# Soft mixture of experts: slot products ahead of both experts' halves, a mix in 32-column blocks, the tokens' maxima moved into the steps

## The chip, the cores and the metric

One core of one Trainium2 chip runs the whole kernel as one launch. The metric is the device time of one execution in microseconds (us); below a time is the median of its runs.

## The reference, cut to what matters

The kernel computes four pairs of attention and feed-forward layers on 32 batches of 64 tokens (2048 tokens) of 128 features. The change touches one of the eight, the soft mixture of experts of the third pair, on 64 experts with 32 slots each (2048 slots):

```python
logits = jnp.einsum('bmd,dnp->bmnp', x, phi)              # 32 x 64 tokens, 64 experts, 32 slots
dispatch = jax.nn.softmax(logits, axis=0)                 # over the 32 batches
combine = jax.nn.softmax(logits.reshape(bsz, m, n * p), axis=-1).reshape(bsz, m, n, p)
slots = jnp.einsum('bmd,bmnp->bnpd', x, dispatch)
y = jnp.einsum('bnpd,nde->bnpe', slots, W) + b[None, :, None, :]
out = jnp.einsum('bnpd,bmnp->bmd', y, combine)
```

`x` is the normalised input, and `out` is added to the residual. The softmax of `dispatch` needs, for each position and slot, a maximum over the 32 batches; that of `combine` needs one maximum for each token over all 2048 slots. The tokens lie in 16 tiles of 128 (two batches each).

## The kernel before, in words

`soft_moe` has the five engines as five programs, each in its own written order, joined by counting semaphores; an engine waits at each instruction whose data or buffer isn't ready, and everything behind it on that engine waits too. It works in `I` = 8 chunks of 256 slots (8 experts). In chunk `i`:

- The stage of logits. TensorE computes the logits of the chunk ahead, j = i + 1, in eight products `logits(j, k)` (L1794) of two token tiles each into the two banks `slot_ps`, and between them transposes chunk i's weights `comb` (`turn`, L1816). ScalarE copies each out of its bank (`take_logits` L1927, `take_turned` L1931). VectorE's `survey(j, k)` takes the tokens' maxima by a reduction (L2063) and the slots' running maxima `high` by an elementwise maximum against the bank (L2055). `conclude` (L2071 to L2076) folds them into `tall`, `neg` (minus the running maximum of each token over the chunks so far) and `gap` (the step of it).
- Eight steps of slots, g = 0 to 7, one for each pair of token tiles. `fill_slots(i, g)` (L1833) makes the slots' inputs into both `slot_ps` banks; ScalarE copies them out (`take_slots`, L1939); `experts(i, g, c)` (L1847) multiplies with the weights of four experts, c = 0 and 1 being the two halves; VectorE adds the bias (`take_experts`, L2129); `mix(i, g)` (L1861) sums the experts' outputs for the tokens, and VectorE's `add` (L2145) adds that to `acc` with the rescaling of earlier chunks.
- Inside the steps the chunk ahead is prepared: ScalarE's `exp_comb(j, k)` (L1949), four exponentials with sums, k = 0 to 3; GpSimd's `lower(j, k)` (L2019), which subtracts the slots' maxima `peak`; ScalarE's `exp_spread(j, k)` (L1959); VectorE's `add_up` (L2109); then `swap_part` (L1808), `invert`, and GpSimd's four `share` (L2024) in the stage of logits.

`fill_slots(i, g)` waits until `take_slots(i, g - 1)` is through, `experts(i, g, c)` until the slots are copied and the bank's last content is taken, `mix(i, g)` until both halves have their bias. TensorE's order in the steps is

```python
for g in range(1, 8):
    experts(i, g - 1, 0)
    if g == (1 if i else 2) and ahead:
        swap_tall(i + 1)
    fill_slots(i, g)
    experts(i, g - 1, 1)
    if g >= 2:
        mix(i, g - 2)
```

The last chunk has nothing ahead; VectorE's `invert_tokens` (L2152 to L2159), small operations on 128x16, stands between `add(i - 1, 7)` and its steps.

Of the kernel before, what the change touches and what calls it, by code (L numbers as in the profile page):

```python
# [1711 lines left out]
def soft_moe(nc, core):  # L1712
# [7 lines left out]
    with Step(nc, "soft") as st:  # L1720
# [48 lines left out]
        wide = lambda v: v[:].unsqueeze(1).broadcast_to([128, 4, SC])  # L1769

# [11 lines left out]
        def _(pe):  # L1782
            def logits(j, k):
                if k >= 2:
                    pe.wait_ge(logit_taken, 8 * j + k - 1)
                    if j >= 2 and k >= 3:
                        pe.wait_ge(high_step, 7 * j + k - 2)
                elif j >= 2:
                    pe.wait_ge(slot_taken, 8 * (j - 1))
                elif j == 1:  # L1790
                    pe.wait_ge(logit_taken, 8)
                for tt in range(2):
                    t = 2 * k + tt
                    last = nc.tensor.matmul(slot_ps[k % 2][:, tt, :], core.xnT[:, 128 * t:128 * t + 128],  # L1794
                                            phi[:, 2 * j:2 * j + 2, :], start=True, stop=True)
                last.then_inc(logit_done, 1)
# [55 lines left out]
            def mix(i, g):  # L1852
# [5 lines left out]
                for tt in range(2):  # L1858
                    for c in range(2):
                        for h in range(2):  # L1860
                            last = nc.tensor.matmul(mix_ps[64 * h:64 * h + 64, tt, :],  # L1861
                                                    combT[:, c, 2 * g + tt, 64 * h:64 * h + 64], outs[u % 3][:, c, h, tt, :],
                                                    start=(c == 0), stop=(c == 1))
# [16 lines left out]
            for i in range(I):  # L1880
# [9 lines left out]
                if i:  # L1890
                    mix(i - 1, 7)
# [30 lines left out]
        def _(act):  # L1922
            def take_logits(j, k):
# [3 lines left out]
                nc.scalar.activation(spread[j % 2][:, 2 * k:2 * k + 2, :], slot_ps[k % 2][:], ACT.Copy).then_inc(logit_taken, 1)  # L1927
# [25 lines left out]
            def exp_gap(j):  # L1953
                act.wait_ge(gap_done, j)
# [22 lines left out]
            for i in range(I):  # L1977
# [8 lines left out]
                for g in range(8):  # L1986
# [3 lines left out]
                    if ahead:  # L1990
# [56 lines left out]
        def _(dve):  # L2047
# [9 lines left out]
            def survey(j, k):  # L2057
# [3 lines left out]
                if j >= 2:  # L2061
                    heighten(j, k, slot_ps[k % 2][:])
# [4 lines left out]
            def conclude(j):  # L2067
# [3 lines left out]
                nc.vector.tensor_tensor(tall[:], high[:, 0, :], high[:, 1, :], ALU.max).then_inc(tall_done, 1)  # L2071
                dve.wait_ge(own_done, 8 * j + 8)
# [121 lines left out]
            for i in range(I):  # L2194
# [6 lines left out]
                if i and ahead:  # L2201
                    survey(i + 1, 0)
                    survey(i + 1, 1)
                if i:
                    add(i - 1, 7)
                if i and ahead:
                    for k in range(2, 8):
                        survey(i + 1, k)
                    conclude(i + 1)
                if not ahead:  # L2210
                    invert_tokens()
                for g in range(1, 8):
                    take_experts(i, g - 1, 0)
                    if g == (1 if i else 2) and ahead:
                        take_peak(i + 1)
# [399 lines left out]
```

## Time and profile before

| | |
|---|---|
| median of 3 runs | 1032.79 us (1032.47 to 1032.89) |
| span of the profiled execution, first to last instruction | 1031.8 us |
| profiled execution's time outside its span | not recorded; the runs' median is 1.0 us above the span |
| mean granted TensorE clock | 0.942 of full speed |
| soft mixture, first `swap_part` to last `mix` | 542.9 to 913.1 us |
| one whole chunk inside it | 46.8 us |

The page gives each engine's busy share over the span; views of a stretch give the same for one stage, and the timeline gives the instructions in the order of time. Columns of a timeline row are start, length, engine, line, operation, output and input with their shapes, the number merged into the row, and in brackets the idle time before it with what ended it. A row that merges many matmuls ends when the last has drained, which overlaps the start of the next.

### The profile page before, as it was taken

How to read it: one execution, taken by the hardware profiler on the slowest of the kernel's cores; microseconds unless marked ns; L12 is line 12 of the kernel's file. 1: busy time of each engine (PE TensorE's matmuls, PEld its weight loads, DVE VectorE, ACT ScalarE, POOL GpSimd, SP SyncE). 2: the span in 40 equal slices, each digit the busy share in tenths (PEclk: the TensorE clock that was granted, in tenths of full speed). 3: DMA queues.
4: the chain of work that ended last, by engine and by line, in shares of the span. 5: the costliest groups of instructions: out<-in, count | busy, mean ns of one | idle time of the engine just before them, and what ended most of it. 6: DMA issues, size and time to landing. Idle time of an engine off the chain costs nothing. (4 is left out here: it accounts for less than half of the span.)

```text
span 1031.8 us, 26604 instructions
## 1 busy us (share of the span) xinstructions
PE 857.6 (83%) x10453; PEld 625.7 (61%) x10453; DVE 749.6 (73%) x1825; ACT 572.7 (56%) x1316; POOL 437.1 (42%) x286
## 2 busy tenths in 40 slices
PE   4274798889739996889878999999999999878888
PEld 3152554778526775545556777777777776644567
DVE  4989787678765544688797758576776758589974
ACT  4172244567615553467687484756648484246774
POOL 5000220597226776198205343342516253509820
PEclk9587899899959999899979999999999999899999
DMA  5411000400051112200010000000000000000001
GB/s 161 123 50 82 1 1 1 171 2 2 17 223 46 52 52 63 59 1 2 3 50 2 27 3 27 3 27 3 27 15 14 28 2 3 2 2 1 2 2 41
DMA packets 27127, 35.95 MB, mean 35 GB/s; under 512 B 7835, under 2 KB 20444, under 8 KB 26238
## 3 DMA queue, kind: packets, MB, share of 16 engines
q1 hardware_dynamic: 21310, 27.84, 8.4%
q0 software_dynamic: 2496, 5.12, 1.8%
q8 instruction: 85, 1.39, 0.6%
q10 hardware_dynamic: 3200, 1.31, 0.5%
q14 instruction: 36, 0.29, 0.1%
HBM read 26.98 MB, written 7.27 MB: 33 GB/s over the span
## 5 line engine op out<-in xcount | busy, mean ns | idle before, releaser
L2129 DVE TENSOR_TENSOR soft_outs<-soft_expert_ps,soft_bias 128x512 f32<-128x512 f32 x128 | 87.3, 688 | 89.5 <-PE soft_expert_ps L1847 89.5
L1847 PE MATMUL soft_expert_ps<-soft_W,soft_slots 128*32 128x128 f32 x4096 | 138.4, 278 | 9.7 <-issue 4.5
L1847 PEld LDWEIGHTS soft_expert_ps<-soft_W,soft_slots 128*32 128x32 f32 x4096 | 106.0, 110 | 40.7 <-issue 37.3
L1939 ACT ACTIVATE soft_slots<-soft_slot_ps 128x512 f32<-128x512 f32 x128 | 69.5, 594 | 85.2 <-PE soft_slot_ps L1833 83.5
L953 POOL TENSOR_TENSOR l_prob<-l_prob,l_inv 128x1024 f32<-128x1024 f32 x48 | 91.3, 1901 | 40.4 <-DVE l_inv L1107 39.0
L2024 POOL TENSOR_TENSOR l_ring<-l_ring,soft_inv 128x1024 f32<-128x1024 f32 x15 | 35.1, 2373 | 106.2 <-DVE soft_inv L2122 57.7
L1092 DVE TENSOR_REDUCE l_under<-l_score 128x16 f32<-128x1024 f32 x48 | 58.8, 1224 | 26.7 <-PE l_score L1173 14.4
L1794 PE MATMUL soft_slot_ps<-phi,xnT 128*128 128x256 f32 x256 | 69.3, 408 | 7.4 <-ACT soft_spread L1927 4.7
L1861 PE MATMUL soft_mix_ps<-soft_outs,soft_combT 128*64 128x128 f32 x1024 | 70.1, 279 | 1.5 <-DVE soft_acc L2145 1.5
L982 PE MATMUL l_turned<-ident,l_prob 128*128 128x128 f32 x384 | 52.4, 279 | 21.9 <-POOL l_prob L953 21.9
L1056 ACT ACTIVATE l_probT<-l_turned 128x512 f32<-128x512 f32 x96 | 52.1, 594 | 33.2 <-PE l_turned L982 33.2
L2024 POOL TENSOR_TENSOR soft_spread<-soft_spread,soft_inv 128x1024 f32<-128x1024 f32 x16 | 37.4, 2372 | 73.9 <-DVE soft_inv L2122 73.9
L1861 PEld LDWEIGHTS soft_mix_ps<-soft_outs,soft_combT 128*64 128x64 f32 x1024 | 54.7, 137 | 15.4 <-issue 13.8
L982 PEld LDWEIGHTS l_turned<-ident,l_prob 128*128 128x128 f32 x384 | 41.1, 140 | 33.5 <-POOL l_prob L953 33.3
L1794 PEld LDWEIGHTS soft_slot_ps<-phi,xnT 128*128 128x128 f32 x256 | 48.0, 202 | 18.0 <-ACT soft_spread L1927 5.8
L1101 DVE TENSOR_REDUCE l_total<-l_prob 128x16 f32<-128x1024 f32 x48 | 58.0, 1208 | 0.1
L1351 POOL DMA_INDIRECT xn_tok<-moe_rows,expert_source x39 | 37.8, 970 | 44.3 <-DVE expert_target L1588 32.7
L2019 POOL TENSOR_TENSOR soft_spread<-soft_spread,soft_peak 128x1024 f32<-128x1024 f32 x16 | 37.9, 2377 | 27.7 <-ACT l_values L1949 27.7
L1096 DVE TENSOR_TENSOR l_shifted<-l_score,l_under 128x768 f32<-128x768 f32 x48 | 46.0, 957 | 1.6
L1493 ACT ACTIVATE expert_rings<-expert_turned 128x512 f32<-128x512 f32 x39 | 23.3, 597 | 42.2 <-PE expert_turned L1394 42.2
L1355 POOL DMA_INDIRECT moe_back<-xnT,expert_target x39 | 38.4, 985 | 19.0 <-DVE xnT L1616 10.4
L1046 ACT ACTIVATE l_prob<-l_shifted 128x768 f32<-128x768 f32 x48 | 40.6, 845 | 10.6 <-DVE l_shifted L1096 10.6
(450 smaller groups left out, 2174.4 us busy)
## 6 DMA issues: line engine op xcount, KB each, us to landing
moe_w<-in_moe_W SPq DMA_DIRECT2D x2, 2048.0 KB, 10.1
soft_W<-in_soft_W SPq DMA_DIRECT2D x16, 256.0 KB, 2.8
kept<-early SPq DMA_DIRECT2D x1, 2048.0 KB, 6.3
l_keys<-in_moe_b SPq DMA_DIRECT2D x1, 2048.0 KB, 8.2
l_asked<-kept SPq DMA_DIRECT2D x1, 2048.0 KB, 13.0
ctxT<-in_ctxT SPq DMA_DIRECT2D x1, 1024.0 KB, 5.1
moe_rows<-xn_tok SPq DMA_DIRECT2D x4, 256.0 KB, 3.7
expert_rings<-moe_back SPq DMA_DIRECT2D x4, 256.0 KB, 6.1
```

The lines of the kernel that those rows point to most:

```text
L953: nc.gpsimd.tensor_tensor(prob[t % 4][:], prob[t % 4][:], inv[t % 2][:].unsqueeze(2).broadcast_to(S16), ALU.mult).then_inc(share_done, 1)
L982: last = nc.tensor.transpose(turned[j][:, k, :], prob[t % 4][:, 2 * m:2 * m + 2, :], core.ident[:])
L1056: nc.scalar.activation(probT[t % 2][:, 4 * j:4 * j + 4, :], turned[j][:], ACT.Copy).then_inc(done, 1)
L1092: nc.vector.tensor_reduce(under[t % 2][:], scores[t % 2][:], AX.X, ALU.max, negate=True).then_inc(top_done, 1)
L1096: nc.vector.tensor_tensor(shifted[t % 2][:], scores[t % 2][:, 0:KEEP, :], under[t % 2][:, 0:KEEP].unsqueeze(2).broadcast_to([128, KEEP, S] ...
L1101: nc.vector.tensor_reduce(total[t % 2][:], prob[t % 4][:], AX.X, ALU.add).then_inc(total_done, 1)
L1794: last = nc.tensor.matmul(slot_ps[k % 2][:, tt, :], core.xnT[:, 128 * t:128 * t + 128], phi[:, 2 * j:2 * j + 2, :], start=True, stop=True)
L1847: last = nc.tensor.matmul(expert_ps[c][32 * j:32 * j + 32, h, tt, :], slots[u % 3][:, h, tt, 128 * c + 32 * j:128 * c + 32 * j + 32], W[i ...
L1861: last = nc.tensor.matmul(mix_ps[64 * h:64 * h + 64, tt, :], combT[:, c, 2 * g + tt, 64 * h:64 * h + 64], outs[u % 3][:, c, h, tt, :], sta ...
L1939: last = nc.scalar.activation(slots[u % 3][:, h], slot_ps[h][:], ACT.Copy)
L2024: nc.gpsimd.tensor_tensor(spread[j % 2][:, quarter(k), :], spread[j % 2][:, quarter(k), :], wide(inv), ALU.mult).then_inc(share_done, 1)
L2129: nc.vector.tensor_tensor(outs[u % 3][:, c].rearrange("p h t d -> p (h t) d"), expert_ps[c][:].rearrange("p h t d -> p (h t) d"), bias[i % ...
```

## The change

Four edits in `soft_moe`, for chunks i >= 1 unless said otherwise:

1. In each step `fill_slots(i, g)` comes first, then both experts' halves of g - 1, then `mix(i, g - 2)` (all chunks). `mix` is cut into blocks of 32 columns: 32 weight loads and matmuls in place of 16.
2. `mix(i - 1, 7)` moves from the start of the stage of logits to behind `fill_slots(i, 0)`, and `swap_tall(i + 1)` to behind `turn(i, 7)`.
3. Logits of later chunks go through four banks: `slot_ps` and, for k % 4 >= 2, `expert_ps`.
4. VectorE keeps only the slots' maxima in the stage of logits (`survey_slots`, `heighten_last`). The tokens' maxima move into the steps: `survey_tokens(i + 1, g)` for g = 0 to 3, each with its quarter of `neg` and `gap`. `exp_comb(i + 1, g)` now waits for its own quarter; `exp_gap` and `exp_spread` come one step later.

```diff
 # TensorE
-                if k >= 2:
+                if j >= 2:
+                    if k >= 4:
+                        pe.wait_ge(logit_taken, 8 * j + k - 3)
+                        if k >= 5:
+                            pe.wait_ge(high_step, 7 * j + k - 4)
+                    elif k >= 2:
+                        pe.wait_ge(expert_taken, 16 * (j - 2) + 15 + k - 2)
+                    else:
+                        pe.wait_ge(slot_taken, 8 * (j - 1))
+                elif k >= 2:
                     pe.wait_ge(logit_taken, 8 * j + k - 1)
...
-                        for h in range(2):
-                            last = nc.tensor.matmul(mix_ps[64 * h:64 * h + 64, tt, :],
-                                                    combT[:, c, 2 * g + tt, 64 * h:64 * h + 64], outs[u % 3][:, c, h, tt, :],
-                                                    start=(c == 0), stop=(c == 1))
+                        for j in range(4):
+                            last = nc.tensor.matmul(mix_ps[32 * j:32 * j + 32, tt, :],
+                                                    combT[:, c, 2 * g + tt, 32 * j:32 * j + 32], outs[u % 3][:, c, j // 2, tt, :],
+                                                    start=(c == 0), stop=(c == 1), tile_position=(0, 32 * j))
...
                 if i:
-                    mix(i - 1, 7)
                     for k in range(7):
...
                 fill_slots(i, 0)
+                if i:
+                    mix(i - 1, 7)
                 turn(i, 7)
+                if i and ahead:
+                    swap_tall(i + 1)
                 for g in range(1, 8):
+                    fill_slots(i, g)
                     experts(i, g - 1, 0)
-                    if g == (1 if i else 2) and ahead:
-                        swap_tall(i + 1)
-                    fill_slots(i, g)
                     experts(i, g - 1, 1)
                     if g >= 2:
                         mix(i, g - 2)
+                    if g == 2 and not i:
+                        swap_tall(1)
 # ScalarE
-                elif k == 0:
-                    act.wait_ge(neg_done, j + 1)
-                    act.wait_ge(turn_done, 8 * j)
+                else:
+                    act.wait_ge(neg_done, neg_by(j, k))
+                    if k == 0:
+                        act.wait_ge(turn_done, 8 * j)
...
-                        if h == 0:
+                        if h == (4 if i else 0):
                             exp_gap(i + 1)
-                        if 2 <= h < 6:
-                            exp_spread(i + 1, h - 2)
+                        low = h - 3 if i else h - 2
+                        if 0 <= low < 4:
+                            exp_spread(i + 1, low)
 # VectorE
+            def survey_tokens(j, k):
+
+                survey(j, 2 * k)
+                survey(j, 2 * k + 1)
+                dve.wait_ge(own_done, 8 * j + 2 * k + 2)
+                nc.vector.tensor_tensor(neg[:, j, quarter(k)], neg[:, j - 1, quarter(k)], own[:, j, quarter(k)], ALU.min).then_inc(neg_done, 1)
+                dve.wait_ge(neg_done, neg_by(j, k))
+                nc.vector.tensor_tensor(gap[:, j, quarter(k)], neg[:, j, quarter(k)], neg[:, j - 1, quarter(k)], ALU.subtract).then_inc(gap_done, 1)
...
                 if i and ahead:
-                    survey(i + 1, 0)
-                    survey(i + 1, 1)
+                    for k in range(8):
+                        survey_slots(i + 1, k)
+                    heighten_last(i + 1)
                 if i:
                     add(i - 1, 7)
                 if i and ahead:
-                    for k in range(2, 8):
-                        survey(i + 1, k)
-                    conclude(i + 1)
+                    survey_tokens(i + 1, 0)
+                    take_peak(i + 1)
...
+                    if i and ahead and g < 4:
+                        survey_tokens(i + 1, g)
```

## Rows read from the trace of the kernel before

**Rows 1.** The page, busy time of each engine over the whole span.
```profile
PE 857.6 (83%) x10453; PEld 625.7 (61%) x10453; DVE 749.6 (73%) x1825; ACT 572.7 (56%) x1316; POOL 437.1 (42%) x286
```

**Rows 2.** Windows, seven steps of one chunk: length, busy (instructions) by engine, clock, DMA, GB/s.
```profile
690.00:723.70 33.70, 32.89 (x694) 25.19 (x694) 19.56 (x40) 20.88 (x54) 9.50 (x4) 1.00 0.01 3
```

**Rows 3.** Timeline, TensorE: start, length, engine, line, operation; `swap_part` of two chunks.
```profile
676.93 0.70 PE L1808 MATMUL soft_swap_ps<-soft_part,halves 128*128 128x256 f32 x2
...
723.74 0.70 PE L1808 MATMUL soft_swap_ps<-soft_part,halves 128*128 128x256 f32 x2
```

**Rows 4.** Timeline, TensorE, one step of slots.
```profile
707.48 1.09 PE L1861 MATMUL soft_mix_ps<-soft_outs,soft_combT 128*64 128x128 f32 x16
708.50 1.08 PE L1847 MATMUL soft_expert_ps<-soft_W,soft_slots 128*32 128x128 f32 x32
709.51 1.13 PE L1833 MATMUL soft_slot_ps<-soft_spread,xn_tok 64*128 64x256 f32 x8
710.58 1.08 PE L1847 MATMUL soft_expert_ps<-soft_W,soft_slots 128*32 128x128 f32 x32
711.59 1.09 PE L1861 MATMUL soft_mix_ps<-soft_outs,soft_combT 128*64 128x128 f32 x16
```

**Rows 5.** Timeline, TensorE, both experts' halves without a slot product between.
```profile
720.83 1.95 PE L1847 MATMUL soft_expert_ps<-soft_W,soft_slots 128*32 128x128 f32 x64
...
722.72 1.09 PE L1861 MATMUL soft_mix_ps<-soft_outs,soft_combT 128*64 128x128 f32 x16
```

**Rows 6.** Timeline, the stage of logits up to the first slot product.
```profile
724.28 1.89 PE L1794 MATMUL soft_slot_ps<-phi,xnT 128*128 128x256 f32 x8
...
732.84 1.03 PE L1794 MATMUL soft_slot_ps<-phi,xnT 128*128 128x256 f32 x4
...
733.71 0.60 PE L1816 MATMUL soft_turn_ps<-ident,l_values 128*128 128x128 f32 x4
...
734.14 1.03 PE L1794 MATMUL soft_slot_ps<-phi,xnT 128*128 128x256 f32 x4
...
735.84 0.69 DVE L2055 TENSOR_TENSOR soft_high<-soft_high,soft_slot_ps 128x512 f32<-128x512 f32 x1
...
736.67 1.13 PE L1833 MATMUL soft_slot_ps<-l_ring,xn_tok 64*128 64x256 f32 x8 [0.63 <-POOL l_ring L2024]
```

**Rows 7.** Timeline, ScalarE, one step with its exponentials.
```profile
702.47 1.09 ACT L1939 ACTIVATE soft_slots<-soft_slot_ps 128x512 f32<-128x512 f32 x2
...
703.45 0.51 ACT L1949 ACTIVATE l_values<-l_ring,soft_neg 128x256 f32<-128x256 f32 x1
...
705.41 1.05 ACT L1959 ACTIVATE l_ring<-l_ring 128x1024 f32<-128x1024 f32 x1
```

**Rows 8.** Timeline, VectorE: an addition, a reduction, the tokens' minimum.
```profile
712.73 0.61 DVE L2145 SCALAR_TENSOR_TENSOR soft_acc<-soft_acc,soft_scale,soft_mix_ps 128x128 f32<-128x128 f32 x2 [0.31 <-PE soft_mix_ps L1861]
...
729.93 0.68 DVE L2063 TENSOR_REDUCE soft_own<-soft_spread 128x2 f32<-128x512 f32 x1
...
730.52 0.68 DVE L2055 TENSOR_TENSOR soft_high<-soft_high,soft_slot_ps 128x512 f32<-128x512 f32 x1
...
737.37 0.17 DVE L2074 TENSOR_TENSOR soft_neg<-soft_neg,soft_own 128x16 f32<-128x16 f32 x1
```

**Rows 9.** Timeline, GpSimd's shares beside small VectorE operations.
```profile
867.70 9.33 POOL L2024 TENSOR_TENSOR soft_spread<-soft_spread,soft_inv 128x1024 f32<-128x1024 f32 x4 [19.22 <-DVE soft_inv L2122]
...
870.12 2.29 DVE L2155 TENSOR_TENSOR soft_token<-soft_token,soft_scale 128x16 f32<-128x16 f32 x1
```

**Rows 10.** Timeline and windows, TensorE after long idle time.
```profile
443.08 1.09 PE L982 MATMUL l_turned<-ident,l_prob 128*128 128x128 f32 x8 [1.66 <-POOL l_prob L953]
...
880.33 1.94 PE L1847 MATMUL soft_expert_ps<-soft_W,soft_slots 128*32 128x128 f32 x32 [3.32 <-DVE soft_outs L2129]
...
880.30:886.00 5.70, 5.67 (x72) 4.08 (x72) 1.17 (x2) 1.09 (x2) 5.50 (x6) 0.50 0.00 0
...
927.19 1.98 PE L1672 MATMUL l_score<-l_ring,xn_tok 64*64 64x512 f32 x8 [2.15 <-ACT l_prob L1048]
```

More of the change, by code:

```diff
@@ L1769, in soft_moe @@
         wide = lambda v: v[:].unsqueeze(1).broadcast_to([128, 4, SC])
+        apart = [bank[:].rearrange("p h t d -> p h (t d)") for bank in expert_ps]
+        logit_bank = lambda j, k: apart[k % 2] if j >= 2 and k % 4 >= 2 else slot_ps[k % 2][:]
+        neg_by = lambda j, k: j + 1 if j < 2 else 4 * (j - 2) + k + 3
+        gap_by = lambda j: j if j < 2 else 4 * (j - 1) + 1
         @block.sync
@@ L1783, in logits @@
             def logits(j, k):
-                if k >= 2:
+                if j >= 2:
[8 more added lines that the diff above has]
+                elif k >= 2:
                     pe.wait_ge(logit_taken, 8 * j + k - 1)
[L1786 to L1789, printed above, removed]
                 elif j == 1:
@@ L1793, in logits @@
                     t = 2 * k + tt
-                    last = nc.tensor.matmul(slot_ps[k % 2][:, tt, :], core.xnT[:, 128 * t:128 * t + 128],
+                    last = nc.tensor.matmul(logit_bank(j, k)[:, tt, :], core.xnT[:, 128 * t:128 * t + 128],
                                             phi[:, 2 * j:2 * j + 2, :], start=True, stop=True)
@@ L1926, in take_logits @@
                     act.wait_ge(slot_done, 8 * (j - 1))
-                nc.scalar.activation(spread[j % 2][:, 2 * k:2 * k + 2, :], slot_ps[k % 2][:], ACT.Copy).then_inc(logit_taken, 1)
+                nc.scalar.activation(spread[j % 2][:, 2 * k:2 * k + 2, :], logit_bank(j, k), ACT.Copy).then_inc(logit_taken, 1)
             def take_turned(i, k):
@@ L1953, in exp_gap @@
             def exp_gap(j):
-                act.wait_ge(gap_done, j)
+                act.wait_ge(gap_done, gap_by(j))
                 nc.scalar.activation(scale[:, j, :], gap[:, j, :], ACT.Exp).then_inc(scale_done, 1)
@@ L2060, in survey @@
                 dve.wait_ge(logit_taken, 8 * j + k + 1)
-                if j >= 2:
-                    heighten(j, k, slot_ps[k % 2][:])
                 nc.vector.tensor_reduce(own[:, j, 2 * k:2 * k + 2], here, AX.X, ALU.max, negate=True).then_inc(own_done, 1)
@@ L2065, in survey, with survey_slots, heighten_last @@
                     heighten(j, k, here)
-            def conclude(j):
+            def survey_slots(j, k):
+                dve.wait_ge(logit_taken, 8 * j + k + 1)
+                heighten(j, k, logit_bank(j, k))
+            def survey_tokens(j, k):
[5 more added lines that the diff above has]
+                nc.vector.tensor_tensor(gap[:, j, quarter(k)], neg[:, j, quarter(k)], neg[:, j - 1, quarter(k)], ALU.subtract).then_inc(gap_done, 1)
+            def heighten_last(j):
                 dve.wait_ge(high_step, 7 * j + 7)
@@ L2071, in conclude @@
                 nc.vector.tensor_tensor(tall[:], high[:, 0, :], high[:, 1, :], ALU.max).then_inc(tall_done, 1)
+            def conclude(j):
+                heighten_last(j)
                 dve.wait_ge(own_done, 8 * j + 8)
@@ L2213, in _ @@
                     take_experts(i, g - 1, 0)
-                    if g == (1 if i else 2) and ahead:
-                        take_peak(i + 1)
+                    if g == 2 and not i:
+                        take_peak(1)
                     if i == 0 and g == 1:
```

## The prediction

> **What bounds the kernel now.** I first read the busy shares of the page: TensorE is the busiest engine with 83%, VectorE follows with 73% [rows 1]. Those are averages over stages, so I went to the windows of the stage that the change touches. In the steps of one chunk TensorE is busy for 32.89 of 33.70 us at a granted clock of 1.00, VectorE for 19.56 and ScalarE for 20.88 [rows 2]: here TensorE is the bound, and only its own instructions, the gaps between them, or a wait put in their place can move the time. The timeline of TensorE then gives the frame: from one `swap_part` to the next 46.81 us [rows 3], of which 12.93 lie between `swap_part` and `fill_slots(i, 0)` [rows 3, 6] (the stage of logits), and so 33.88 from there to the next `swap_part` (the steps). Six chunks (i = 1 to 6) repeat this; the first and the last are special.
>
> A step takes 4.11 us [rows 4], start to start: experts to slots 1.01, slots to experts 1.07, experts to mix 1.01, and mix to experts 1.02. Two expert halves one behind the other take 1.89 until the mix starts, so 0.88 for the first and 1.01 for the second [rows 5]: leaving one shape of tile for another costs some 0.13 us.
>
> **The change part by part.** All sums are made against this execution, span 1031.8 us, which stands 1.0 us under the median of 1032.79; I carry differences over to the median.
>
> *Order in the steps and 32-column mix.* Slots, half, half, mix is 1.07 + 0.88 + 0.88 + 1.01 = 3.84 us, 0.27 less, if the mix follows the experts as one half follows the other and keeps TensorE as long. Its 32 pieces of 32 columns have the shape of one half of the experts, and a half and a 64-column mix take the same time now (1.01 and 1.02), so I take 0.88 + the switch. Bounds: no more than a mix and its switch today (1.02, so 0.14 more in each step that TensorE bounds), no less than 0.84, since the same columns stream. No trace row shows a mix of this shape. The Trainium skill (TensorEngine Tiling (Array Packing), Key Properties) says that a change of tiling mode drains the engine while a change of tile doesn't; by it, too, this mix would follow without a drain.
>
> *Stage of logits, chunks 1 to 6.* Now summed for after: `swap_part` to the first logits 0.54, two logits 1.73, five rounds of logits and transposes of 1.30 (732.84 to 734.14), and 2.53 from the last logits to the first slot product: its drain, ScalarE's copy, VectorE's maximum, which ends at 736.53 and releases `fill_slots` [rows 6]. Together 11.30 against 12.93: 1.6 us less for each chunk. This last wait stays as it is, since slot products still wait for all eight copies and maxima. What goes is `mix(i - 1, 7)` and its two switches, and a third of a microsecond of waiting for `high`. The third logits now wait for `take_experts(i - 1, 7, 0)`, over 1 us earlier by my schedule: nothing.
>
> *Maxima in the steps, chunks 1 to 6.* Here a new ring of waits closes. I count from the start of `fill_slots(i, g)`. TensorE starts `mix(i, g - 2)` 2.83 later and ends it at 3.92. Behind it VectorE adds from 3.97 (two instructions, 0.53 until the next can start), reduces twice (0.60 each to the next start, 0.68 for the last), and forms `neg` (0.17 and some 0.04 for the semaphore) [rows 8]: 5.98. `exp_comb(i + 1, g)` starts 0.04 later and holds ScalarE for 1.96 [rows 7]; only behind it stands `take_slots(i, g + 1)`, 1.09 [rows 7]; then `fill_slots(i, g + 2)` can start 0.13 later (as 735.84 + 0.69 to 736.67, [rows 6]). That is 9.2 us for two steps, 4.6 each, where TensorE needs 3.84 and the old order took 4.11. In the old order the exponentials waited for nothing inside the steps.
>
> GpSimd makes it longer. `neg` and `gap` have both inputs in SBUF. Beside GpSimd's four shares (2.33 each) such an operation of 128x16 took 2.29 us, ending where the current share ended; with GpSimd idle it takes 0.17 [rows 8, 9]. In the steps `lower(i + 1, k)` (L2019) has a share's shape, which I take at a share's 2.33, and starts about 0.2 behind `exp_comb(i + 1, k)`, so the next `neg` is out no earlier than 2.56 behind those exponentials. The Trainium skill (SBUF — State Buffer, Who interferes with whom) gives this as a rule: a VectorE instruction with two SBUF inputs contends with GpSimd's reads, and the later one blocks fully. The trace agrees; if it did not hold here, the sum below would be 0.7 us a chunk shorter.
>
> The schedule, from the start of `fill_slots(i, 0)`: `mix(i - 1, 7)` 1.07, `turn` 2.10, `swap_tall` 2.54, `fill_slots(1)` 3.17, experts 4.24 and 5.12. VectorE: `add(i - 1, 7)` 2.21, the first `neg` 4.24. (`tall` stands behind the last share until about 1.6; `swap_tall` needs it at 2.5: hidden under the mix, 0.) `exp_comb(0)` 4.28 to 6.36; `take_slots(1)` 6.25 to 7.34; `fill_slots(2)` 7.47, where TensorE was ready at 6.13. `neg(1)` would be out at 8.36 and is held by `lower(0)` until 8.92; `exp_comb(1)` ends at 11.04, `fill_slots(3)` 12.15. The same again, 4.68 later each: `fill_slots(4)` 16.83, `exp_comb(3)` ends 20.40. Behind it `exp_spread(0)` takes 1.04 more [rows 7] before `take_slots(4)`, so `fill_slots(5)` 22.55, where TensorE was ready at 20.7. From there TensorE bounds: 3.84 each, `fill_slots(7)` 30.23, then slots, four halves and two mixes 6.47 to `swap_part` at 36.70. `add_up(0)` is held by `lower(3)` until about 23.4, VectorE is needed again at 24.7: 0. Against 33.88 this is **2.8 us more** for each chunk.
>
> *First chunk.* No ring, the tokens' maxima stay where they were. Five clean steps give 5 x 0.27 = 1.35; the chain to `swap_part` goes over `add(0, 5)`, whose mix now stands one half (0.76 net) later behind its slots: 0.6 to 0.8 less.
>
> *Last chunk.* `invert_tokens` now stands behind an `add(6, 7)` that comes after the slot product. Of it the first operations wait for share ends either way [rows 9], so the stall of TensorE, which ended at 880.33, ends some 0.4 later. But the next slot product, 2.0 us at the half clock of 0.50 behind that stall [rows 10], now runs ahead of it, and four or five steps save 0.27: 2.4 less, with 0.3 lost in VectorE's tail.
>
> *Sum:* 6 x (2.8 - 1.6) - 0.7 - 2.4 = +4.1: span 1035.9, median **1036.9 us**.
>
> **The rivals.** *The ring is shorter than my sum.* If `neg` slips in ahead of `lower`, or semaphores are quicker, a chunk loses 0.7 us of what I add: 6 x 0.7 = 4.2, 1032.7, no change. For it: my `neg` 2 and 3 miss a free GpSimd by only 0.1 to 0.2. Against: [rows 9]. *It doesn't bind (the other side).* If two steps of the ring took 7.68 or less, 1.5 below my count, TensorE would bound all steps: 3.17 + 2.96 + 5 x 3.84 + 6.47 = 31.8, so 2.1 less than 33.88 in each chunk; with 1.6 from the logits 6 x 3.7 + 3.1 = 25 us less, 1007. It decides at `take_slots(i, g + 1)`; half of that shortening would give some 1022. Against it stands that each part of the ring has its row. *The clock falls.* Ahead of `fill_slots(5)` TensorE idles for about 1.8 us. Behind 1.66 us of idling its matmuls kept their length (1.09 for eight), behind 2.15 and 3.32 they took twice that, and the clock was 0.50 for 5.7 us behind the latter [rows 10], 2.9 lost. In all six chunks that is 17 us: 1054; in one or two, 1040 to 1043. TensorE doing less than I think in the steps makes that likelier. *The 32-column mix is not quicker.* 0.14 in some 28 to 35 steps that TensorE bounds: 4 to 5 us, 1041.
>
> **Chances.** The forecast 0.56 (own range 1033 to 1041, which is 0.7 us a chunk either way); the shorter ring 0.14; not binding 0.12; clock 0.12; mix not quicker 0.06. The range 1029 to 1045 holds the forecast, the shorter ring, the mix, and single falls of the clock; it leaves out most of "not binding" and the full loss of clock. Within 0.2% (1030.7 to 1034.9, about what a measurement of this kernel can tell from no change) lie the shorter ring and a little of the forecast: 0.19. Slower: the rest of the forecast, clock, mix, 0.67. Faster 0.14.
>
> **What would show it.** In the trace after: steps 5 to 7 of a chunk at 3.84 us; `swap_part` to the first slot product 11.3; in steps 1 to 4 `exp_comb` waiting for `neg`, `take_slots` late behind it with nothing to wait for, and `fill_slots` waiting for ScalarE, starts 4.7 apart; `neg` operations of 0.5 us and more instead of 0.17; GpSimd's `lower` 4.7 apart. TensorE's busy share in the steps falls to about 85%. Wrong it would be if VectorE got through its reductions before the mix, if `exp_comb` were out of the way sooner, or if a clock below 1.00 stood in the windows of chunks 1 to 6.

## Result and the profile after

Slower, by about as much as its measurement can tell: 1035.88 us (median of 13 runs, 1034.50 to 1037.33) against 1033.36 us for the kernel before (13 runs, 1032.31 to 1035.70), a ratio of 1.0023 with a 95% interval of 1.0014 to 1.0031. The profiled execution has a span of 1032.5 us and its own time is 1034.5 us, the lowest of the 13. So the spans of the two profiled executions lie only 0.7 us apart where the medians lie 2.5 apart; what follows accounts for the 0.7.

In the profile of the changed kernel the lines of `soft_moe` stand some 9 lines (TensorE) to 29 (end of VectorE's program) further down. First the page of the changed kernel, its busy time by engine:

```profile
PE 832.9 (81%) x11477; PEld 630.6 (61%) x11477; DVE 780.2 (76%) x1861; ACT 572.7 (55%) x1316; POOL 436.4 (42%) x286
```

TensorE has 1024 more instructions and 24.7 us less busy time than in [rows 1]. Of these, 21.3 us lie between the first `swap_part` and the next layer's first scores (357.0 before, 335.7 now). Most of that is the 0.29 us by which TensorE's own work in each of the 64 steps became shorter (3.82 for 4.11), through fewer switches of tile shape; a smaller part is matmuls that ran at half clock before and no longer do. Yet the time did not fall. The windows of one chunk of the changed kernel say where it went, first the steps, then the stage of logits:

```profile
688.70:725.00 36.30, 31.82 (x838) 26.99 (x838) 29.58 (x55) 21.07 (x55) 11.26 (x5) 1.00 0.01 3
677.38:688.68 11.30, 10.67 (x66) 9.30 (x63) 8.49 (x14) 8.08 (x15) 7.48 (x4) 1.00 0.19 58
```

In the steps before, TensorE worked for 32.89 of 33.70 us [rows 2]; now it works for 31.82 of 36.30 and is no longer what bounds them. VectorE has some 10 us more work in the steps (29.58 for 19.56), mostly the reductions that moved there. The granted clock is 1.00 in both. The timeline of the changed kernel over that chunk (compare [rows 3, 4, 6, 7]) shows what TensorE waits for:

```profile
677.38 0.70 PE L1817 MATMUL soft_swap_ps<-soft_part,halves 128*128 128x256 f32 x2
...
688.68 1.13 PE L1842 MATMUL soft_slot_ps<-soft_spread,xn_tok 64*128 64x256 f32 x8 [0.63 <-DVE soft_high L2069]
...
691.78 1.13 PE L1842 MATMUL soft_slot_ps<-soft_spread,xn_tok 64*128 64x256 f32 x8
...
695.15 2.35 POOL L2033 TENSOR_TENSOR l_ring<-l_ring,soft_peak 128x1024 f32<-128x1024 f32 x1 [4.61 <-ACT l_values L1962]
...
696.11 1.14 PE L1842 MATMUL soft_slot_ps<-soft_spread,xn_tok 64*128 64x256 f32 x8 [1.31 <-ACT soft_slots L1951]
696.77 0.75 DVE L2089 TENSOR_TENSOR soft_neg<-soft_neg,soft_own 128x4 f32<-128x4 f32 x1
...
697.55 0.51 ACT L1962 ACTIVATE l_values<-l_ring,soft_neg 128x256 f32<-128x256 f32 x1 [1.59 <-DVE soft_neg L2089]
...
699.53 1.05 ACT L1951 ACTIVATE soft_slots<-soft_slot_ps 128x512 f32<-128x512 f32 x2
699.77 2.37 POOL L2033 TENSOR_TENSOR l_ring<-l_ring,soft_peak 128x1024 f32<-128x1024 f32 x1 [2.27 <-ACT l_values L1962]
...
700.73 1.14 PE L1842 MATMUL soft_slot_ps<-soft_spread,xn_tok 64*128 64x256 f32 x8 [0.73 <-ACT soft_slots L1951]
701.90 0.26 DVE L2089 TENSOR_TENSOR soft_neg<-soft_neg,soft_own 128x4 f32<-128x4 f32 x1
...
705.37 1.14 PE L1842 MATMUL soft_slot_ps<-soft_spread,xn_tok 64*128 64x256 f32 x8 [0.75 <-ACT soft_slots L1951]
...
710.95 1.14 PE L1842 MATMUL soft_slot_ps<-soft_spread,xn_tok 64*128 64x256 f32 x8 [1.68 <-ACT soft_slots L1951]
...
714.77 1.14 PE L1842 MATMUL soft_slot_ps<-soft_spread,xn_tok 64*128 64x256 f32 x8
...
725.03 0.70 PE L1817 MATMUL soft_swap_ps<-soft_part,halves 128*128 128x256 f32 x2
```

Read it as a ring. The bracket of a slot product (L1842) names ScalarE's copy of the slots (L1951) as what it waited for. But that copy, at 699.53, has no wait of its own: it stands behind four exponentials, whose first (697.55) waited 1.59 us for `neg` (L2089). `neg` ended at 697.52, right where GpSimd's `lower` of the round before ended (695.15 + 2.35 = 697.50), and the next `neg` at 702.16 where the next `lower` ended (699.77 + 2.37 = 702.14). One round is 4.64 us. The hold itself is long only in the first round: `neg` took 0.75, 0.26 and 0.27 us for 0.16, so in the later two it was held for 0.1 us only. From 710.95 on the slot products are 3.82 us apart. All of it together, the idle time ahead of the slot products in the whole kernel (us, times):

```profile
its engine sat idle before it (us, times) until:
...
  ACT soft_slots L1951: 28.1, 25
```

That is four times in each of the six chunks, and once more. The last chunk, timeline of the changed kernel (against [rows 10]):

```profile
879.80 1.14 PE L1842 MATMUL soft_slot_ps<-soft_spread,xn_tok 64*128 64x256 f32 x8
...
884.80 2.52 PE L1856 MATMUL soft_expert_ps<-soft_W,soft_slots 128*32 128x128 f32 x64 [3.87 <-DVE soft_outs L2158]
887.03 2.00 PE L1870 MATMUL soft_mix_ps<-soft_outs,soft_combT 128*32 128x128 f32 x32
888.96 1.36 PE L1842 MATMUL soft_slot_ps<-soft_spread,xn_tok 64*128 64x256 f32 x8
```

Now the slot product (879.80) runs ahead of the stall, at full clock, and the half clock behind it costs 1.7 us (2.52, 2.00 and 1.36 for what takes 1.95, 1.06 and 1.14 elsewhere) where it cost 2.9.

| part, profiled executions | before | after | difference |
|---|---|---|---|
| up to the first `swap_part` | 542.88 | 542.61 | -0.27 |
| first chunk | 40.45 | 39.67 | -0.78 |
| six chunks | 280.85 | 285.70 | +4.85 (47.6 for 46.8 each) |
| last chunk, to the next layer's first scores | 57.81 | 54.86 | -2.95 |
| from there to the end | 109.8 | 109.7 | -0.15 |

### The profile page after: what moved, and what is told of

It reads as the page before. It is cut to its first block and busy times, and to the rows that moved or that the text cites. A ratio compares the mean times of both kernels' runs of the same rounds, so it can differ in the third digit from the quotient of the medians.

```text
span 1032.5 us, 28676 instructions
## 1 busy us (share of the span) xinstructions
PE 832.9 (81%) x11477; PEld 630.6 (61%) x11477; DVE 780.2 (76%) x1861; ACT 572.7 (55%) x1316; POOL 436.4 (42%) x286
## 5 line engine op out<-in xcount | busy, mean ns | idle before, releaser
L1856 PE MATMUL soft_expert_ps<-soft_W,soft_slots 128*32 128x128 f32 x4096 | 125.7, 275 | 4.8 <-DVE soft_outs L2158 4.8
L1856 PEld LDWEIGHTS soft_expert_ps<-soft_W,soft_slots 128*32 128x32 f32 x4096 | 108.9, 110 | 23.6 <-issue 23.6
L1951 ACT ACTIVATE soft_slots<-soft_slot_ps 128x512 f32<-128x512 f32 x128 | 68.6, 586 | 54.5 <-PE soft_slot_ps L1842 54.5
L1870 PE MATMUL soft_mix_ps<-soft_outs,soft_combT 128*32 128x128 f32 x2048 | 69.1, 275 | 1.0 <-DVE soft_acc L2174 1.0
L1870 PEld LDWEIGHTS soft_mix_ps<-soft_outs,soft_combT 128*32 128x32 f32 x2048 | 57.7, 111 | 3.7 <-issue 3.6
L1842 PE MATMUL soft_slot_ps<-l_ring,xn_tok 64*128 64x256 f32 x256 | 36.3, 400 | 17.6 <-ACT soft_slots L1951 14.8
L1842 PE MATMUL soft_slot_ps<-soft_spread,xn_tok 64*128 64x256 f32 x256 | 36.5, 402 | 16.0 <-ACT soft_slots L1951 13.2
L1803 PE MATMUL soft_slot_ps<-phi,xnT 128*128 128x256 f32 x160 | 43.6, 419 | 6.5 <-ACT soft_spread L1939 4.6
```

What stands on the lines that cost most here:

```text
L1842: last = nc.tensor.matmul(slot_ps[h][:, tt, :], core.xn[rows, t, :], spread[i % 2][rows, t, :], start=True, stop=True)
L1856: last = nc.tensor.matmul(expert_ps[c][32 * j:32 * j + 32, h, tt, :], slots[u % 3][:, h, tt, 128 * c + 32 * j:128 * c + 32 * j + 32], W[i ...
L1870: last = nc.tensor.matmul(mix_ps[32 * j:32 * j + 32, tt, :], combT[:, c, 2 * g + tt, 32 * j:32 * j + 32], outs[u % 3][:, c, j // 2, tt, :] ...
L1951: last = nc.scalar.activation(slots[u % 3][:, h], slot_ps[h][:], ACT.Copy)
```

## The experiments

A chunk below is the time from one `swap_part` to the next, in the middle of the stage. All ratios are to the kernel before, run on the same chip. The chunk is the cleaner of the two measures. In four of the profiled executions (64-column mix; exponentials a step later; both of the last two; `gap` by quarters) the granted clock fell to between 0.78 and 0.87 for the 30 us behind the next layer's first scores, and from those scores to the end they took 112.4 to 112.6 us, where all others took 109.7 to 110.2. Whether these falls belong to the edits isn't shown, so up to 2.9 us of a difference in time may lie outside the stage. The first of these stretches of 10 us in the kernel with the 64-column mix (window: length, busy by engine, clock):

```profile
912.12:922.12 10.00, 6.78 (x55) 3.65 (x56) 8.68 (x9) 4.56 (x11) 4.92 (x3) 0.78 0.00 1
```

| kernel | median us | ratio to before (95%) | one chunk us |
|---|---|---|---|
| before | 1033.36 | 1 | 46.81 |
| the change | 1035.88 | 1.0023 (1.0014 to 1.0031) | 47.65 |
| order and mix alone | 1015.46 | 0.9829 (0.9814 to 0.9844) | 44.70 |
| the same, 64-column mix | 1026.33 | 0.9927 (0.9910 to 0.9944) | 45.59 |
| change, all maxima back in the stage of logits | 1015.48 | 0.9825 (0.9808 to 0.9842) | 44.25 |
| change, exponentials a step later | 1022.13 | 0.9892 (0.9876 to 0.9907) | 44.97 |
| change, maxima into PSUM | 1031.85 | 0.9980 (0.9971 to 0.9989) | 46.99 |
| change, maxima ahead of the addition | 1034.40 | 1.0009 (0.9996 to 1.0022) | 47.64 |
| both of the last two | 1028.45 | 0.9951 (0.9934 to 0.9967) | 46.20 |
| exponentials later, PSUM, `gap` once | 1007.74 | 0.9745 (0.9729 to 0.9762) | 42.90 |
| exponentials later, PSUM, `gap` by quarters | 1010.95 | 0.9775 (0.9758 to 0.9791) | 43.28 |
| later, PSUM, `gap` once, and `invert_tokens` later | 1018.12 | 0.9844 (0.9828 to 0.9861) | 42.90 |
| the same, and GpSimd waits for it | 1019.20 | 0.9720 (0.9705 to 0.9734) | 42.90 |

### Which part of the change does what

*The step order and the 32-column mix alone*, in the kernel before; maxima, banks and `mix(i - 1, 7)` stay as they were:

```diff
-                        for h in range(2):
...
+                        for j in range(4):
...
                 turn(i, 7)
+                if i and ahead:
+                    swap_tall(i + 1)
                 for g in range(1, 8):
+                    fill_slots(i, g)
                     experts(i, g - 1, 0)
-                    if g == (1 if i else 2) and ahead:
-                        swap_tall(i + 1)
-                    fill_slots(i, g)
                     experts(i, g - 1, 1)
...
```

> The kernel before with the first edit alone: in each step the slot product first, then both experts' halves, then the mix in 32-column blocks; swap_tall behind turn(i, 7). Maxima, two banks and mix(i - 1, 7) stay as before. My theory (the order gains, the ring of waits in the steps eats it): the exponentials wait for nothing here, so steps run at 3.82 us, fill_slots(i, 0) to swap_part falls from 33.9 to about 31.4, the stage of logits stays at 12.9, a chunk 44.3; time 1015 us. Rival (the 32-column mix or the new order itself costs): steps at 4.1 us or more, time 1033 or above.

1015.46 us. A chunk is 2.11 us shorter, the six together 13.0; the first chunk gives 0.8 (39.68), the last 5.2 (850.77 to 903.38), and 0.8 is lost outside them. The steps came out as expected (31.5), the stage of logits at 13.2 us for 12.9. This part of the change is worth 18 us.

*The same with the old two blocks of 64 columns in `mix`:*

```diff
-                        for j in range(4):
-                            last = nc.tensor.matmul(mix_ps[32 * j:32 * j + 32, tt, :],
...
+                        for h in range(2):
+                            last = nc.tensor.matmul(mix_ps[64 * h:64 * h + 64, tt, :],
```

> The kernel before with the new order in the steps but its old mix in two 64-column blocks. My theory: the switch between the experts' shape and the mix's costs 0.13 us each time and there are 8 to 9 more of them in a chunk, so a step is 3.96 instead of 3.82 us, a chunk 45.8 instead of 44.7, time 1024 (the same order with 32 columns: 1015.5). Rival (the blocks don't matter, the order alone gains): 1015 to 1016.

1026.33. Timeline of this kernel, one step:

```profile
665.29 1.95 PE L1847 MATMUL soft_expert_ps<-soft_W,soft_slots 128*32 128x128 f32 x64
667.17 1.09 PE L1861 MATMUL soft_mix_ps<-soft_outs,soft_combT 128*64 128x128 f32 x16
668.20 1.13 PE L1833 MATMUL soft_slot_ps<-l_ring,xn_tok 64*128 64x256 f32 x8
669.26 1.96 PE L1847 MATMUL soft_expert_ps<-soft_W,soft_slots 128*32 128x128 f32 x64
```

and the same step of the changed kernel:

```profile
715.83 1.95 PE L1856 MATMUL soft_expert_ps<-soft_W,soft_slots 128*32 128x128 f32 x64
717.60 1.06 PE L1870 MATMUL soft_mix_ps<-soft_outs,soft_combT 128*32 128x128 f32 x32
718.59 1.13 PE L1842 MATMUL soft_slot_ps<-soft_spread,xn_tok 64*128 64x256 f32 x8
```

From the experts to the mix it takes 1.88 us against 1.77, from the mix to the slots 1.03 against 0.99. The mix in the experts' shape follows them 0.11 us sooner, and the slots follow it 0.04 sooner: 3.97 against 3.82 a step. A chunk is 0.89 us longer, the six together 5.6. The rest of the difference of about 10 (0.9927 less 0.9829, of 1033.4) lies in the first chunk (0.7), in the last (54.71 against 52.61, where the clock fell, see below), and in the next layer: 2.2 us in the profiled executions, with a granted clock of 0.78, 0.84 and 0.87 in the three stretches of 10 us behind its first scores, against 1.00, 0.83 and 1.00 with the 32-column mix. By an estimate from these rows some 7 us of the difference come from the shape itself, and 3 to 4 stand beside the lower clock (1.5 of them at the row of 3.47 us shown at the end); whether the shape brings the lower clock about isn't shown.

*The change with all the maxima back in the stage of logits* (four banks, order, mix and the place of `mix(i - 1, 7)` kept; `exp_gap` and `exp_spread` go back to their old steps with them):

```diff
-                    heighten_last(i + 1)
+                        survey(i + 1, k)
+                    conclude(i + 1)
...
-                    survey_tokens(i + 1, 0)
...
-                    if i and ahead and g < 4:
-                        survey_tokens(i + 1, g)
```

> The changed kernel with the tokens' maxima back in the stage of logits (all eight reductions and one neg there, exponentials as before), order, four banks, 32-column mix and mix(i - 1, 7) as changed. My theory: VectorE now paces the stage of logits (1.2 us for each of eight), swap_part to the first slot product 11.95 instead of 11.30, but no ring in the steps: 32.2 instead of 36.35, a chunk 44.1, time 1014. Rival (something else in the changed order costs): the steps stay at 35 or more, time 1033 or above.

1015.48, and a chunk of 44.25. Taken as differences between neighbouring kernels, the chunk's +0.84 has three parts: order and mix -2.11, four banks with the later `mix(i - 1, 7)` -0.45, tokens' maxima in the steps +3.40. The last is +4.27 in the steps (36.35 for 32.08) and -0.86 in the stage of logits (11.30 for 12.16). Six times 3.40 is 20.4 us, and the timed medians differ by the same 20.4; the profiled spans differ by 18.7, since this kernel's stage began 1.9 us later in its execution. Of the 2.5 that the banks gain in the six chunks against the first experiment, 2.05 were lost in the last chunk (54.66 for 52.61, a stall of 3.89 with the half clock behind it); the timed medians are equal.

### What closes the ring

Two closed chains of waits were possible. One goes over TensorE: mix, addition, maxima, `neg`, exponentials, copy of the slots, slot product. The other does without it: `neg`, exponentials, `lower`, which holds up the next `neg`.

*Maxima into PSUM*: the reductions of quarters 1 to 3 write to `swap_ps`, so `neg` has one input in SBUF and one in PSUM.

```diff
-                nc.vector.tensor_reduce(own[:, j, 2 * k:2 * k + 2], here, ...
+                nc.vector.tensor_reduce(swap_ps[:, 0, 2 * k:2 * k + 2] if j >= 2 and k >= 2 else own[...], here, ...
...
+                if k:
+                    dve.wait_ge(peak_done, j + 1)
```

> The changed kernel with the tokens' maxima of quarters 1 to 3 written to PSUM (the first half of swap_ps, free behind peak), so that the minimum for neg has one input in SBUF and one in PSUM; gap stays as it is. If GpSimd's lower holds up an operation with two SBUF inputs: neg takes 0.17 us instead of 0.75, 0.26 and 0.27, the ring is 0.8 us shorter in a chunk, chunk 46.85, 4.7 us less than the changed kernel, 1031. Rival (neg is late for another reason): no change, 1036. If the hold were the whole loss of the steps, fill_slots(i, 0) to swap_part would fall to 32; my theory says it stays near 35.5.

1031.85. Timeline of this kernel:

```profile
695.58 2.36 POOL L2033 TENSOR_TENSOR l_ring<-l_ring,soft_peak 128x1024 f32<-128x1024 f32 x1 [4.60 <-ACT l_values L1962]
...
696.54 1.13 PE L1842 MATMUL soft_slot_ps<-soft_spread,xn_tok 64*128 64x256 f32 x8 [1.31 <-ACT soft_slots L1951]
697.22 0.16 DVE L2091 TENSOR_TENSOR soft_neg<-soft_neg,soft_swap_ps 128x4 f32<-128x4 f32 x1
...
705.71 1.13 PE L1842 MATMUL soft_slot_ps<-soft_spread,xn_tok 64*128 64x256 f32 x8 [1.23 <-ACT soft_slots L1951]
```

`neg` takes 0.16 us in the middle of `lower`, so the hold came from its second input in SBUF. The chunk is 0.66 shorter, where the prediction gave 0.7. But from 696.54 to 705.71 two steps still take 9.17 us. The longer chain, over TensorE, was counted at 9.2 in the prediction and is nearly as long as two rounds of the other (9.28). Taking one of them away shows the other.

*Maxima ahead of the addition* in VectorE's order, in steps 2 and 3, which shortens the chain over TensorE alone; as an edit of the change, and then on top of the maxima in PSUM:

```diff
+                    if i and ahead and g < 4:
+                        survey_tokens(i + 1, g)
                     if g >= 2:
...
-                    if i and ahead and g < 4:
-                        survey_tokens(i + 1, g)
```

> The changed kernel with survey_tokens(i + 1, g) ahead of add(i, g - 2) in steps 2 and 3 on VectorE. My theory: in the changed kernel neg(2) and neg(3) end when GpSimd's lower ends, so starting them 0.53 us sooner changes nothing: chunk 47.6, 1036. Rival (the addition is in the ring that sets the time): 0.5 us less a chunk, 47.1, 1033.

> The same order (survey_tokens ahead of the addition) on the kernel with the maxima in PSUM, which measured 1031.85 us and a chunk of 46.98. There GpSimd no longer holds neg. My theory: now the addition is in the ring, neg(3) comes 0.53 us sooner and with it the fifth slot product: chunk 46.45, 1028.7. Rival (something else holds the ring): chunk 46.98, 1032.

Alone it leaves the chunk at 47.64: the hold sets the pace. With the hold gone it takes 0.79 us off the chunk (46.99 to 46.20). That is more than the 0.53 expected, because the maxima then wait neither for the addition nor for the mix in front of it: from the step's last bias addition to its first reduction it was 1.39 us (699.63 to 701.02) and is 0.60 (696.74 to 697.34). The hold and the chain are both real, and each covers the other.

*Exponentials one step later*: ScalarE forms `exp_comb(i + 1, k)` behind the slots' copy of step k + 1, so nothing in the same step waits for them.

```diff
-                        h = g if i else g - 1
+                        h = g - 1
...
-                        if h == (4 if i else 0):
+                        if h == (3 if i else 0):
                             exp_gap(i + 1)
-                        low = h - 3 if i else h - 2
+                        low = g - 3
```

> The changed kernel with exp_comb(i + 1, k) one step later on ScalarE (behind take_slots(i, k + 1) instead of in front of it); VectorE and TensorE untouched, so the tokens' maxima stay in the steps and GpSimd still holds them up. My theory (what costs is that the copy of the slots stands behind exponentials that wait for neg): fill_slots no longer waits, fill_slots(i, 0) to swap_part 31.6 us instead of 36.35, a chunk 42.9, time 1007. Rival (VectorE's extra work in the steps, or GpSimd's hold on it, is the cost by itself): the chunk stays at 46 to 47.6, time 1030 to 1036.

1022.13, 15 us above what was expected. Timeline of this kernel:

```profile
691.44 2.38 POOL L2033 TENSOR_TENSOR l_ring<-l_ring,soft_peak 128x1024 f32<-128x1024 f32 x1 [5.62 <-ACT l_values L1962]
692.08 1.77 DVE L2089 TENSOR_TENSOR soft_neg<-soft_neg,soft_own 128x4 f32<-128x4 f32 x1
...
693.88 0.51 ACT L1962 ACTIVATE l_values<-l_ring,soft_neg 128x256 f32<-128x256 f32 x1 [1.59 <-DVE soft_neg L2089]
...
696.10 2.37 POOL L2033 TENSOR_TENSOR l_ring<-l_ring,soft_peak 128x1024 f32<-128x1024 f32 x1 [2.28 <-ACT l_values L1962]
...
696.99 1.50 DVE L2089 TENSOR_TENSOR soft_neg<-soft_neg,soft_own 128x4 f32<-128x4 f32 x1
...
698.52 0.51 ACT L1962 ACTIVATE l_values<-l_ring,soft_neg 128x256 f32<-128x256 f32 x1 [1.61 <-DVE soft_neg L2089]
...
699.44 1.96 PE L1856 MATMUL soft_expert_ps<-soft_W,soft_slots 128*32 128x128 f32 x64 [0.64 <-DVE soft_outs L2158]
```

The chain over TensorE is open now, and that gives 2.68 us a chunk (44.97 for 47.65). But the ring of the hold still runs at 4.64 (693.88 to 698.52): `neg` is held longer, 1.77 and 1.50 us, the exponentials wait as before, and VectorE's bias additions behind `neg` come late for TensorE (0.64 us at 699.44). My expectation had let go of that ring, which the prediction had written down.

*Both taken away, and `gap` formed once, in step 5*, when `lower` is through; and the same with `gap` left as it was:

```diff
...
-                nc.vector.tensor_tensor(gap[:, j, quarter(k)], neg[:, j, quarter(k)], neg[:, j - 1, quarter(k)], ALU.subtract)...
...
+                    if i and ahead and g == 5:
+                        dve.wait_ge(neg_done, neg_by(i + 1, 3))
+                        nc.vector.tensor_tensor(gap[:, i + 1, :], neg[:, i + 1, :], neg[:, i, :], ALU.subtract)...
```

> The changed kernel with three edits: exp_comb(i + 1, k) one step later on ScalarE, the tokens' maxima of quarters 1 to 3 in PSUM, and gap formed once for all 16 tiles in step 5 (exp_gap in step 6). With the exponentials alone moved, the trace showed another ring: neg waits for the end of lower(k - 1), exp_comb for neg, lower for exp_comb, 4.64 us a round. My theory: with both rings open TensorE bounds all steps at 3.82 us, fill_slots(i, 0) to swap_part 31.6, a chunk 42.9, time 1007 to 1009. Rival (VectorE's work in steps 1 to 3, 3.6 us each, is itself too much): a chunk of 44 or more, 1015 or more.

> Exponentials one step later and maxima of quarters 1 to 3 in PSUM, but gap in each quarter as in the changed kernel (two SBUF inputs, so GpSimd still holds it and the work behind it on VectorE). My theory: nothing on TensorE's path waits for gap, VectorE runs under 1 us late and has that much slack: chunk 42.9 to 43.1, 1008. Rival (any operation that GpSimd holds costs its hold): chunk 44.6 as with neg held, 1018 or more.

1007.74: TensorE bounds every step. Timeline of this kernel:

```profile
686.94 1.13 PE L1842 MATMUL soft_slot_ps<-soft_spread,xn_tok 64*128 64x256 f32 x8
...
690.76 1.14 PE L1842 MATMUL soft_slot_ps<-soft_spread,xn_tok 64*128 64x256 f32 x8
...
694.58 1.13 PE L1842 MATMUL soft_slot_ps<-soft_spread,xn_tok 64*128 64x256 f32 x8
```

3.82 us from `fill_slots(2)` on, and 31.60 from the first slot product to `swap_part`. That is the time that the prediction gave the rival "it doesn't bind" (1007). `gap` by quarters has both inputs in SBUF and is held in its turn: 1.58 us at 690.19 and 1.32 at 698.21, for 0.16. That costs 0.38 us a chunk (43.28, where I had expected 42.9 to 43.1), 2.3 in six; the time is 3.2 us longer (1010.95), and this is one of the executions with the lower clock in the next layer.

### The last chunk

In all these kernels TensorE stalls once in the last chunk, behind `invert_tokens`. *That block moved behind `take_experts` of step 1*, on top of the fastest kernel so far:

```diff
-                if not ahead:
-                    invert_tokens()
                 for g in range(1, 8):
...
+                    if not ahead and g == 1:
+                        invert_tokens()
```

> The kernel with both rings open (1007.74 us), and in the last chunk invert_tokens moved behind the bias additions of step 1 instead of ahead of them. There TensorE idled for 3.89 us behind the third slot product and ran the next three groups at half clock. My theory: GpSimd's shares are over by then, so the 16 small operations take 3.3 us beside TensorE's work; the idle time goes, the clock stays at 1.00: 3.9 + 2.8 = 6.7 us less, 1001. Rival (VectorE is late anyway and the idle time only moves): 1006 to 1008.

1018.12, worse by 10 us. Timeline of this kernel:

```profile
854.46 4.04 DVE L2181 COPY soft_token<-soft_sums 128x16 f32<-128x16 f32 x1
...
854.95 3.52 POOL L159 MEMSET l_values<- 128x4096 f32 x1
...
858.53 4.19 POOL L165 COPY l_values<-l_asked 64x1024 f32<-64x1024 f32 x4
858.74 0.90 DVE L2186 TENSOR_TENSOR soft_token<-soft_token,soft_sums 128x16 f32<-128x16 f32 x1
...
862.80 7.47 POOL L185 TENSOR_TENSOR l_ring<-l_asked,head_of 128x1024 f32<-128x1024 f32 x4
...
864.78 1.82 DVE L2184 TENSOR_TENSOR soft_token<-soft_token,soft_scale 128x16 f32<-128x16 f32 x1
...
871.91 3.64 PE L1856 MATMUL soft_expert_ps<-soft_W,soft_slots 128*32 128x128 f32 x64 [13.24 <-DVE soft_outs L2158]
```

I had expected 1001. The block now falls into GpSimd's next work. Its copy is out only when the share and the MEMSET behind it have both ended (858.47), and the small operations, 0.17 us alone, take up to 0.95 and 1.82 beside GpSimd's copies and products. TensorE idles for 13.24 us.

*The same, with GpSimd waiting until the block is through:*

```diff
             pool.wait_ge(turn_done, 8 * I)
+            pool.wait_ge(token_step, 2 * I)
             queries.lay_apart(pool)
```

> As the kernel with invert_tokens behind step 1's bias additions, which measured 1018.12 us, but GpSimd waits for the end of invert_tokens before it lays the next layer's queries apart (its memset, copies and products). In the trace of that kernel the copy of 128x16 took 4.04 us, until the memset ended, and eight of the small two-input operations 0.9 to 1.8 us each beside GpSimd's copies and products. My theory: it was only this company that cost; without it the operations take 3.4 us, TensorE idles under 1 us and keeps its clock: 6 us less than the kernel with both rings open (1007.74), 1001 to 1002. Rival (GpSimd's work, now 3 to 4 us later, delays the next layer, or its products hold up VectorE in later steps): 1006 to 1010.

On the chip that ran this one the kernel before took 1048.35 us (9 runs), and this kernel's first `swap_part` comes at 558.70, that of the fastest one at 544.11: the excess lies ahead of the stage. So only ratios compare, 0.9720 against 0.9745, about 2.6 us, with intervals that overlap a little: that it is faster is likely and not shown. Inside the profiles the last chunk takes 51.66 us (855.83 to 907.49) against 55.64 (841.19 to 896.83). Timeline of this kernel:

```profile
868.34 0.60 DVE L2182 COPY soft_token<-soft_sums 128x16 f32<-128x16 f32 x1
...
872.31 3.52 POOL L159 MEMSET l_values<- 128x4096 f32 x1 [3.40 <-DVE soft_token L2189]
872.85 1.95 PE L1856 MATMUL soft_expert_ps<-soft_W,soft_slots 128*32 128x128 f32 x64 [0.30 <-DVE soft_outs L2159]
...
876.26 1.85 DVE L2195 SCALAR_TENSOR_TENSOR x_tok<-soft_acc,soft_token,x_tok 128x128 f32<-128x128 f32 x2
```

The stall shrank to 0.30 us and the clock kept its level, 4.0 us less in the chunk; I had expected 6. GpSimd's work, put later, now holds up VectorE's last additions (1.85 us at L2195 beside GpSimd's copies, 0.61 without), and TensorE waits for VectorE later in the chunk, 1.34 us at 889.55.

## Why the prediction was right, point by point

*The number.* 1035.88 lies 1.0 us under the 1036.9 forecast, and part of that is luck. The sum gave +4.1 us; the medians moved by 2.5 and the profiled spans by 0.7. The sum was 2.2 us too high in the six chunks, 0.6 in the last, 0.1 in the first, and 0.4 of the difference lies outside the stage. Against that, I had added 1.0 us to come from span to median. The executions timed later show 1.8 us between time and span for the kernel before and 2.0 for the changed one, and the median before came out at 1033.36 for 1032.79. So the span forecast, 1035.9, was 2.0 us above that of the median execution (1033.9), and the short step to the median took half of it back.

*Direction and mechanism.* Right. The ring closed where it was said to, in steps 1 to 4 of each chunk, at 4.64 us a round for the 4.68 of the sum, with `exp_comb` waiting for `neg`, the slots' copy late behind it, and a last stall of 1.68 us ahead of `fill_slots(5)` (about 1.8 predicted).

*Order and mix, 3.84 us a step.* 3.82. Taking the mix at the experts' price was right; with 64 columns a step took 0.15 us more, which is the 0.14 of the bound and of the rival "not quicker".

*Stage of logits, 11.30.* 11.30 (677.38 to 688.68), the wait of 0.63 for the last maximum included.

*Maxima in the steps, +2.8 a chunk.* This is the term that was mis-sized: +2.5 (36.35 against 33.88). From `fill_slots(0)` the slot products came at 3.10, 7.43, 12.05, 16.69 and 22.27, where the sum had 3.17, 7.47, 12.15, 16.83 and 22.55: each round a little short. With the stage of logits the net is +0.84 a chunk for +1.2, 2.2 us in six.

*GpSimd's hold, 0.7 a chunk.* 0.66 when it was taken away, though `neg` was held for more than 0.5 us in one round of three only, where the prediction had named 0.5 and more as the sign. The rule of the Trainium skill (SBUF — State Buffer, Who interferes with whom), that an instruction with two SBUF inputs waits out GpSimd's, holds in these steps: 0.75 us for `neg` with both inputs in SBUF, 0.16 with one in PSUM. That either chain is almost as long as the other was in the numbers (9.2 for two steps, two rounds of 4.68) and I did not draw the consequence, that shortening one gives only as much as the other lets through. Without the hold a chunk lost 0.66 us, with the chain over TensorE shortened nothing, with both 1.45. With that chain opened outright it lost 2.68, with both opened 4.75.

*First and last chunk, -0.7 and -2.4.* -0.78 and -2.95. The stall of the last chunk ended 0.7 us later relative to `swap_part` (16.82 for 16.15), where I had said 0.4. The slot product ran ahead of it at full clock, as said, and with it went 0.9 of the 2.9 us that the half clock had cost [rows 10]. What the half clock cost behind the stall was 1.7 us, 0.3 less than the rest, which was not foreseen.

*The clock.* Kept in the six chunks at idle times of 1.68 us, as [rows 10] had it for 1.66. *The rival "not binding"* (0.12) was wrong for this kernel; opening the two chains gave its time to within 1 us, so the price of the ring was right from that side too.

## What to carry over

Before moving work into steps that another engine bounds, write down each closed chain of waits that it adds, over every engine, with the length of one round. Where two are nearly equal, price taking away both, not one. Here a VectorE operation of 0.16 us carried a ring because both its inputs lay in SBUF and GpSimd was busy; writing one input to PSUM, or forming `gap` where GpSimd's `lower` was through, took the hold away. And measure the parts of a change alone: here order, mix and banks together were worth 18 us, and the maxima in the steps cost 20.

## What had not been expected of the hardware

The clock did not go by the length of the idling alone. Ahead of experts' products in the last chunk it kept its level behind an idle time of 2.36 us in the kernel with order and mix alone (64 matmuls 1.95 us), and fell behind one of 2.35 us in the one with the 64-column mix (3.47 us). The granted clock was 1.00 in the former from 865 to 880, and 0.83 in the latter from 870 to 880. First the former, then the latter, from their timelines:

```profile
867.20 1.95 PE L1847 MATMUL soft_expert_ps<-soft_W,soft_slots 128*32 128x128 f32 x64 [2.36 <-DVE soft_outs L2131]
```

```profile
873.55 3.47 PE L1847 MATMUL soft_expert_ps<-soft_W,soft_slots 128*32 128x128 f32 x64 [2.35 <-DVE soft_outs L2131]
```

The same shows in the next layer. Behind 2.15 us of idling a group of eight score matmuls took 1.98 us in the kernel before [rows 10], behind 2.14 in the changed one 1.09, from its timeline:

```profile
928.04 1.09 PE L1672 MATMUL l_score<-l_ring,xn_tok 64*64 64x512 f32 x8 [2.14 <-ACT l_prob L1048]
```

What tells them apart stays open; no run was made for it.

The copy of 128x16 from SBUF to SBUF, with a single input, took 4.04 us and ended with a GpSimd MEMSET (858.50 and 858.47), whose row names no input, while in the changed kernel operations with two inputs ran through a MEMSET at 0.17 us (881.15 to 884 beside 881.02 to 884.53). That this copy was held by a write and the two-input operations were not is read from these two places alone; no run was made for it.
